# Attention block with a mixture of experts: blanks in 19 pieces with result rows of their own, scatters without pauses, the last group's chain dealt anew, joins in 5 parts, mixed order

## The reference

```
h = layernorm(x) * (1 + ca) + sa
q, k, v = split(h @ W_attn + b_attn)                      # 16 heads of 8 channels
att = softmax(q k^T / sqrt(8) + slope_head * (s - t), s <= t only)
x = x + ga * ((att v) @ W_proj + b_proj)
h = layernorm(x) * (1 + cb) + sb
probs = softmax(h @ router_w^T)                           # 8 experts
w, e = top 2 of probs;  w = softmax(w)
y_e = expert_scale[e] * (silu(h @ w1[e]^T) @ w2[e]^T)     # 512 hidden values
x = x + gb * (w_0 y_e0 + w_1 y_e1)
```

## Time and profile before

| | us |
|---|---|
| median of 3 runs | 574.66 (572.46 to 578.66) |
| profiled execution, its own time | 576.61 |
| its span, first to last instruction | 574.8 |
| mean granted clock of PE | 0.919 |
| busy PE, DVE, ACT, POOL | 477.8, 442.8, 384.1, 181.6 |

### The profile page before, as it was taken

The page is one execution under the profiler, slowest core; times in us unless marked ns, Lnnn a source line. Parts: engine busy times, 40 slices in busy tenths (PEclk is TensorE's granted clock), DMA queues, the critical chain, the costliest instruction groups (busy, mean ns, idle before and its releaser), DMA issues.

```text
span 574.8 us, 15827 instructions
## 1 busy us (share of the span) xinstructions
PE 477.8 (83%) x6215; PEld 261.2 (45%) x6215; DVE 442.8 (77%) x760; ACT 384.1 (67%) x747; POOL 181.6 (32%) x336
## 2 busy tenths in 40 slices
PE   3756888889999999999999999998996597799900
PEld 2422333344353454344354344345333587799800
DVE  3689899989999998999998999973877368343303
ACT  3932266668989889889898889886875363355400
POOL 3410000010113111410034101093088857666660
PEclk9965599999999999999999999999879599799965
DMA  5592112000012555242400000100221311122106
GB/s 158 180 325 66 30 34 52 1 3 4 7 35 42 144 234 226 82 157 53 80 10 3 4 2 7 30 7 22 92 71 39 80 53 43 52 66 59 43 22 219
DMA packets 31658, 40.78 MB, mean 71 GB/s; under 512 B 6348, under 2 KB 26768, under 8 KB 30313
## 3 DMA queue, kind: packets, MB, share of 16 engines
q1 hardware_dynamic: 28976, 35.12, 20.8%
q0 software_dynamic: 2272, 4.24, 2.1%
q10 hardware_dynamic: 336, 0.42, 0.2%
HBM read 19.17 MB, written 20.84 MB: 70 GB/s over the span
## 4 chain that ended last, share of the span: by engine, by line
PE 32%; POOL 17%; DVE 12%; issue 7%; ACT 5%; DMA 3%; SPq 1%; POOLq 0%; ACTq 0%; DVEq 0%
PE pv L772 14%; PE b L806 8%; DVE part L1045 8%; POOL y_scratch L1565 6%; PE b L735 5%; POOL slot_scratch L1558 4%; POOL pause L1537 4%; ACT probs L1382 3%; PE b L708 2%; DMA raw<-y_scratch 1%; ACT raw L1349 1%; PE b L884 1%; DMA inverse<-inverse_scratch 1%; POOL raw L1516 1%; POOL yn L1518 1%
## 5 line engine op out<-in xcount | busy, mean ns | idle before, releaser
L1382 ACT ACTIVATE probs<-b 128x512 f32<-128x512 f32 (+1 forms) x576 | 296.1, 571 | 71.3 <-PE b L806 33.8
L1045 DVE TENSOR_REDUCE part<-b 128x2 f32<-128x1024 f32 (+2 forms) x320 | 322.5, 1060 | 21.4 <-PE b L735 9.5
L772 PE MATMUL pv<-probs,v_cur 128*32 128x256 f32 (+1 forms) x2432 | 178.3, 376 | 0.0
L806 PE MATMUL b<-aug 55*128 55x256 bf16 (+1 forms) x1216 | 127.9, 268 | 12.2 <-ACT probs L1382 11.6
L735 PE MATMUL b<-aug 52*128 52x512 bf16 (+3 forms) x640 | 118.1, 367 | 18.6 <-DVE part L1045 16.5
L806 PEld LDWEIGHTS b<-aug 55*128 55x128 bf16 x1216 | 44.5, 95 | 123.9 <-ACT probs L1382 111.0
L772 PEld LDWEIGHTS pv<-probs,v_cur 128*32 128x32 f32 x2432 | 50.4, 109 | 58.5 <-ACT probs L1382 31.3
L735 PEld LDWEIGHTS b<-aug 52*128 52x128 bf16 x640 | 34.6, 95 | 37.4 <-DVE part L1045 27.4
L1565 POOL DMA_INDIRECT y_scratch<-aug,xt x39 | 39.1, 1002 | 30.3 <-POOL pause L1537 30.3
L901 PE MATMUL b<-w2T_sb,hst 128*128 x312 | 43.4, 285 | 3.5 <-DVE aug L1222 2.7
L884 PE MATMUL b<-hTt,aug 128*128 128x128 f32 x312 | 45.0, 291 | 0.0
(11 more groups left out here) (185 smaller groups left out, 375.9 us busy)
## 6 DMA issues: line engine op xcount, KB each, us to landing
slot_scratch<-blank SPq DMA_DIRECT2D x8, 1040.0 KB, 6.7
xt<-slot_scratch SPq DMA_DIRECT2D x39, 65.0 KB, 1.9
aug<-q_scratch SPq DMA_DIRECT2D x6, 384.0 KB
aug<-k_scratch SPq DMA_DIRECT2D x6, 384.0 KB
w2T_sb<-in_w2T SPq DMA_DIRECT2D x1, 2048.0 KB, 10.3
aug<-in_w1T SPq DMA_DIRECT2D x8, 256.0 KB, 2.7
raw<-y_scratch SPq DMA_DIRECT2D x4, 512.0 KB, 5.5
q_scratch<-pieces SPq DMA_DIRECT2D x4, 384.0 KB, 2.6
```

The source lines that it names most:

```text
L772: return mm(pv[32 * hh:32 * hh + 32, c0:c1], v_cur[:, kb, hh, :], probs[:, step_ % 2, hh, at_:at_ + c1 - c0], start=(kb == 0 and c0 == 0), ...
L806: ins = mm(bank[:, at_:at_ + w], k_aug[g % 2][n, pair, kb * P:kb * P + P], q_aug[g % 2][n, pair, j * CW + c0:j * CW + c1], start=True, sto ...
L1045: ins = nc.vector.tensor_reduce(dst, b1[:, slot:slot + 2, at_:at_ + w], AX.X, ALU.max)
L1382: nc.scalar.activation(out, b2[:, (n2 - 1) % RING2, 0:PAIRS * w].rearrange("p (b t) -> p b t", b=PAIRS), ACT.Exp).then_inc(exp_done, 1)
```

## The change

- `blank` is used as two halves. POOL gives every blank row a number of its own, TOPK * T and up, for one of 19 pieces at a time (`number_blanks`), after the transfer of the piece two before has landed; SP sends a piece at each of 19 steps of group 1. `y_scratch` grows from 4,096 to 23,296 rows, `slot_scratch` from 16,512 to 19,200, and the scatter has no bounds check.
- No pause stands ahead of sends and scatters.
- In the last group projections, deviations, routing and counts stand at other steps, and DVE's order is written anew; the send of chunk 0 stands ahead of the deviation of chunk 2. List 1 is made within the tile loop. The late parts of chunk 3 stand one tile earlier.
- The inverse of the sums is taken two steps earlier in each group.
- The end has five parts, of 4, 4, 4, 2 and 2 blocks of 128 tokens.
- In groups 1 to 3, in the steps that hold no diagonal block (24 of 36), one maxima task is interleaved with the scores on PE.

```diff
-SUMS_OUT, SUMS_IN, INVERT, INVERSE_OUT, INVERSE_IN = 3, 4, 8, 9, 10
+SUMS_OUT, SUMS_IN, INVERT, INVERSE_OUT, INVERSE_IN = 3, 4, 6, 7, 8
...
-TABLES_AT, EMPTY_AT, BLANK_AT = 5, [6, 7], [11, 12, 13, 15, 18, 22, 24, 29, 31]
+TABLES_AT, EMPTY_AT = 5, 6
+BLANK_AT = [7, 8, 9, 10, 11, 12, 13, 14, 15, 16, 18, 19, 21, 22, 23, 24, 25, 26, 28]
...
-DEVIATION_AT = {19: 0, 20: 1}
-PROJECT = {16: 0, 18: 1, 23: 2}
+DEVIATION_AT = {17: 0, 20: 1}
+PROJECT = {16: 0, 19: 1, 24: 2}
...
-COUNT = {24: 0, 27: 1, 31: 2}
+COUNT = {21: 0, 26: 1, 33: 2}
...
-SLOT_ROWS = SPARE + P
+SLOT_ROWS = SPARE + MOST * P
...
-PAUSE, GATHER_PAUSE = 512, 224
...
-LATE_PROJECT, LATE_RESIDUAL, LATE_TOKENS, LATE_TURN, LATE_LOGITS, LATE_KEEP = 2, 2, 3, 5, 5, 5
-LATE_EXP, LATE_ROUTE, LATE_COUNT = 6, 6, 8
+LATE_PROJECT, LATE_RESIDUAL, LATE_TOKENS, LATE_TURN, LATE_LOGITS, LATE_KEEP = 1, 1, 2, 4, 4, 4
+LATE_EXP, LATE_ROUTE, LATE_COUNT = 5, 5, 7
+MORE_LIST = {0: (0, 1), 1: (2, 3)}
...
-SENDS_AFTER = 6
+SENDS_AFTER = 5
+LAST_JOINS = [(0, TPC), (TPC, 2 * TPC), (2 * TPC, 3 * TPC), (3 * TPC, NT - 2), (NT - 2, NT)]
...
-        y_dram = nc.dram_tensor("y_scratch", (TOPK * T, C), fp32, kind="Internal").ap()
+        y_dram = nc.dram_tensor("y_scratch", (TOPK * T + SLOT_ROWS, C), fp32, kind="Internal").ap()
...
+                        q = BLANK_AT.index(p)
+                        q0, q1 = HELD * q, min(HELD * (q + 1), EACH)
+                        sp.wait_ge(empty_s, q + 1)
+                        sp.dma_start(slot_dram.rearrange("(p q) c -> p (q c)", p=P)[:, q0 * ROW:q1 * ROW], blank[:, CHUNK * (q % 2):CHUNK * (q % 2) + (q1 - q0) * ROW]).then_inc(blank_out[q % 2], 16)
...
-                def scores_then_maxima(p, b, upto):
-                    alternate(scores(p, b, 0), scores(p, b, 1))
+                def scores_and_maxima(p, b, upto):
+
+                    k, (j, kbs) = at[0], STEPS[p]
+                    if k < upto and not first and kbs[0] < TPC * j:
+                        alternate(chain(scores(p, b, 0), maxima(k, 0, False, True)), chain(maxima(k, 1, True, False), scores(p, b, 1)))
+                        at[0] += 1
+                    else:
+                        alternate(scores(p, b, 0), scores(p, b, 1))
                     pass1(upto)
...
-            list_all(1)
             for j in range(DEEP - 1):
                 stage(j)
...
+                for piece in MORE_LIST.get(j, ()):
+                    list_tiles(1, piece)
...
-            def space_out(columns):
-
-                own.inc(nc.gpsimd.memset(pause[:, 0:columns], 0.0))
-                own.wait()
+            def number_blanks(q):
+
+                if q >= 2:
+                    pool.wait_ge(blank_out[q % 2], 16 * (q // 2))
+                numbers = blank[:, CHUNK * (q % 2):CHUNK * (q % 2 + 1)].rearrange("p (n c) -> p n c", c=ROW)[:, :, 1:2].bitcast(mybir.dt.uint32)
+                nc.gpsimd.iota(numbers, [[1, HELD], [0, 1]], base=TOPK * T + HELD * q, channel_multiplier=EACH).then_inc(empty_s, 1)
...
                 pool.wait_ge(yt_s, j + 1)
-                space_out(GATHER_PAUSE)
                 to = xt[:, j % ROWS_DEEP, 1:2].bitcast(mybir.dt.uint32)
-                nc.gpsimd.indirect_dma_start(y_dram, bass.IndirectOffsetOnAxis(ap=to, axis=0), yt[:, j % OUT_DEEP, :], None, bounds_check=TOPK * T - 1, oob_is_err=False).then_inc(tile_out(j)[0], 16)
+                nc.gpsimd.indirect_dma_start(y_dram, bass.IndirectOffsetOnAxis(ap=to, axis=0), yt[:, j % OUT_DEEP, :], None).then_inc(tile_out(j)[0], 16)
...
+            send_chunk(0)
             deviation(2)
-            for c in range(3):
-                send_chunk(c, PAUSE)
+            send_chunk(1)
+            send_chunk(2)
```

More of the change, by code:

```diff
@@ L13 @@
 from contextlib import ExitStack
-from itertools import zip_longest
+from itertools import chain, zip_longest
 import numpy as np
@@ L397, in build @@
         y_out = [sem(f"y_out{k}") for k in range(OUT_DEEP)]
-        y_in = [sem(f"y_in{c}") for c in range(NC_)]
+        y_in = [sem(f"y_in{m}") for m in range(len(LAST_JOINS))]
         joined = sem("joined")
@@ L831, in step @@
                                 take(pe, rows_in[j % 2], HG * 16)
-                            scores_then_maxima(p, b, min(PLAN[first][p][b], NTASK) if last else PLAN[first][p][b])
+                            scores_and_maxima(p, b, min(PLAN[first][p][b], NTASK) if last else PLAN[first][p][b])
                             if p not in START:
@@ L1222, in keep, with join @@
                 V.scalar_tensor_tensor(yt[:, j % OUT_DEEP, :], b1[:, 2 + j % 2, 0:C], xt[:, j % ROWS_DEEP, 0:1], gate[:, 1, :], ALU.mult, ALU.mult).then_inc(yt_s, 1)
[L1224 to L1229 removed]
+            def join(m):
+                n0, n1 = LAST_JOINS[m]
+                xc = x_sb[:, n0:n1, :]
+                dve.wait_ge(y_in[m], 16)
+                step(V.tensor_tensor(xc, xc, yfin[:, n0:n1, 0, :], ALU.add))
+                V.tensor_tensor(xc, xc, yfin[:, n0:n1, 1, :], ALU.add).then_inc(joined, 1)
             residual(0)
@@ L1233, in _ @@
             residual(1)
-            scale_tokens(1)
             keep_logits(0)
             route(0, 0)
+            scale_tokens(1)
+            for k in range(1, 5):
+                route(0, k)
+            keep_logits(1)
+            route(1, 0)
+            place(0)
+            scale_of(0)
+            weights(0)
             scale_sums(2)
             add_sums(2)
-            keep_logits(1)
-            route(1, 0)
-            for k in range(1, 5):
-                route(0, k)
-            residual(2)
-            place(0)
-            scale_tokens(2)
-            scale_of(0)
-            weights(0)
             for k in range(1, 5):
                 route(1, k)
-            keep_logits(2)
-            route(2, 0)
+            residual(2)
             place(1)
@@ L1286, in _ @@
             keep(TILES - 1)
-            for c in range(NC_):
-                join(c)
+            for m in range(len(LAST_JOINS)):
+                join(m)
         @block.scalar
@@ L1576, in group @@
                             tables()
-                        if p in EMPTY_AT:
-                            q = CHUNK * EMPTY_AT.index(p)
-                            own.inc(nc.gpsimd.memset(blank[:, q:q + CHUNK], 0.0))
+                        if p == EMPTY_AT:
+                            own.inc(nc.gpsimd.memset(blank[:, :], 0.0))
                             own.wait()
-                            numbers = blank[:, q:q + CHUNK].rearrange("p (n c) -> p n c", c=ROW)[:, :, 1:2].bitcast(mybir.dt.uint32)
-                            own.inc(nc.gpsimd.iota(numbers, [[0, TOPK * TPC], [0, 1]], base=TOPK * T, channel_multiplier=0))
-                        if p == EMPTY_AT[-1]:
-                            own.wait()
-                            nc.gpsimd.memset(tick[:, 7:8], 0.0).then_inc(empty_s, 1)
+                        if p in BLANK_AT:
+                            number_blanks(BLANK_AT.index(p))
                         if p == BIAS_AT[0] - 1:
```

74 lines of the change are left out of this document (33 added, 41 removed).

## The result

The median fell from 574.51 to 555.98 us (551.65 to 558.35 over 4 runs); the ratio to the kernel before is 0.966, its 95% interval 0.958 to 0.974. That is a gain of 18.5 us where 27.2 were forecast. The profiled execution has a span of 553.9 us, 6.3 above the forecast sum of 547.6; the median lies 8.5 above the forecast 547.5.

What follows compares the result with a forecast made beforehand. No one engine was taken to bind the whole: PE in middle groups, sends before the experts, POOL's scatters at the end. Last scatter 533.5 plus 14.1 gave 547.6, 27.2 below 574.8; median 574.66 - 27.2 = 547.5 us, range 535 to 560.

Steps and rivals of the forecast that it cites:

- (a): Mixed order of scores and maxima on PE in three groups: gain of 0.5 us per group, -1.5 in all.
- (b): Last group's chain dealt anew: -1 us of a possible 7.3, as moved steps are late as often as early.
- (c): Start of the tile loop: tile 0 starts as attention ends, tile 6 at 462.7 instead of 468.23, gain 5.5 us.
- (d): Tiles 6 to 10, chunk 3's routing: unchanged at 12.5 us, so tile 10 starts at 475.2.
- (e): Tiles 10 to 38: 54.1 us at about PE's own pace instead of 62.8; last up-projection at 529.3.
- (f): Scatters and sends on POOL: 1.1 us each instead of 2.06 between scatters; last scatter at 533.5, not 559.96.
- (g): Blanks numbered in 19 pieces in group 1, and the sums' inverse taken two steps earlier: no cost, 0 us.
- (h): End, from the last scatter's start: 14.1 us instead of 14.84, as the last join handles two token blocks.
- POOL did not keep its wait: First rival, scatters on POOL: the 0.77 us wait belongs to the scatter, not the pause; +5.8, 553 us; chance 0.10.
- scatters did not go by landing: Rival on POOL's queue: each transfer must land before the next, 2.4 us each, 584 us; chance 0.06.
- the numbering did not hold up the maxima: Rival in group 1: waiting for blank pieces to land delays the maxima, +9 us, 556.5 us; chance 0.08.
- the deal cleared nothing: Rival in the last group: the new deal clears all of the 7.3 us instead of 1, 541 us; chance 0.10.

Runs made afterwards that it cites:

- Scaling first: The changed kernel with POOL's second scaling of the last values moved ahead of the first deviation, one step earlier: 551.2 us.
- the projection at step 18: The changed kernel with POOL's second scaling ahead of the first deviation, plus chunk 1's projection one step earlier, at step 18 as before: 547.93 us.
- the plain order: The changed kernel with scores and maxima on PE in the order of before, not interleaved: 555.91 us against 555.98.
- the best version: The changed kernel with POOL's second scaling ahead of the deviation, chunk 1's projection at step 18 and late parts one tile later, routing in one piece: 544.23 us.
- the routing in halves: The best version with chunk 3's routing in two pieces, parts 1 to 3 behind one tile and the rest behind the next: 544.32 us.

## Why the prediction was right, and where not

The time lay in the range and the sign was right, and most of the mechanism: the experts begin when attention ends, POOL no longer lags at the end, and PE sets the pace from tile 10 on. Two of the tests that were to show it wrong came out against it: attention ended later than 440, tile 10 started later than 480. Two of its signs failed by less: scatters stood 1.26 apart where POOL was behind, not 1.0 to 1.2, and the group with the blanks was 0.9 longer than the next.

- (a) and (b) put the last value product at 437.9; it ended at 442.07, 4.2 late. The miss is larger: group 1 began at 165.78 instead of 168.40, 2.6 earlier by chance, since no edit touches what is ahead of it. (a) was small, 0.3 to 0.4 in group 2. The step that failed is (b): "the moved steps are late by a step or two as often as early", so -1. The last group became 4.0 longer. Scaling first took 4.4 of its 99.3 away, the projection at step 18 another 2.7: both shown by a run, with the clock behind each wait in the figure. The order of the change showed POOL's two scalings behind the first deviation, where DVE's tokens start, and I did not ask what shares their time. "What is behind it isn't delayed" was nearly right: the eight sends took 10.6 us, and PE waited 0.91 for the turn of chunk 2.
- (c) was right as a sum: tokens 17.2 us behind the last product (17.7 forecast), tile 6 25.3 (24.8). One reading in it was wrong: of the 8.9 us of waits, 1.05 end at 467.23, behind the stretch from 446.43 to 465.59, so 7.9 were to be taken off. And the 5 us standstill in it was taken as the price of uncovered DVE work. It was the price of one table: with the late parts one tile later, tile 10 comes 6.4 us sooner while the tokens stay where they are.
- (d) was taken as unchanged, 12.5 us; it took 482.13 - 467.36 = 14.8. Behind the same 2.7 us wait PE ran at 0.50 for 5.5 us, which it had not done before, where the same product took 1.15 us instead of 2.07:

```profile
479.41 1.15 PE L901 MATMUL b<-w2T_sb,hst 128*128 x8 [2.72 <-DVE aug L1222]
```

With the scaling and the projection moved, the same loop kept its clock behind this wait (1.00 from 466.6 to 472.1) and took 36.0 - 23.5 = 12.5.
- (e) 53.2 against 54.1, and the last scatter 3.9 us behind the last up-projection against 4.2: right.
- (f) 1.26 us per scatter where 1.1 was taken; 1.26 is the middle value that I had worked out from the sends and passed over. The sends of chunk 3 began at 476.75, not near 471.5, a value for which the prediction gives no working. POOL caught up not at once but at 507.76, which cost nothing.
- (g) the blanks cost nothing, shown above within a microsecond; the earlier inverse was not run by itself. (h) 14.7 against 14.1.

The terms' errors, 4.2 + 0.5 + 2.3 - 0.9 - 0.3 + 0.6 = 6.4, make up the span's 6.3; without the 2.6 of luck ahead of group 1 they are 8.9, near the 8.5 by which the median is off. The rivals: POOL did not keep its wait, scatters did not go by landing, and the numbering did not hold up the maxima; the deal cleared nothing, as it stood. As for scatters beside a copy of weights, which the first rival names: the 13 from 509.65 to 532.40 each have a copy of 0.43 us on DVE within their issue and take 0.96, not 1.19.

What no step asked is which part carries the gain. The pauses alone gave 27.0; that this is almost the 27.2 forecast for the whole is chance. The rest took 7.8 back, through the late parts one tile early (6.4), the scaling behind the deviation (4.8) and the projection one step late (3.3). These three add up to more than the 11.8 that undoing them together gave, and with them undone the remaining parts are worth some 4.0.

## What to carry to other kernels

When a wait is to be removed, remove it by itself first and read the trace before anything else is moved: here the old tables, untouched, fitted the kernel without pauses better than the new ones. An instruction that is moved ahead of its input can become one that its engine stands still for, as PE did here for 5.43 us ahead of the turn of chunk 3. Look for work on POOL and DVE that becomes simultaneous when one of the two is moved (here four token instructions took 3.35 us beside POOL's scaling and 1.4 without it), and price the wait on the engine behind both (PE, 2.17 us).

## What the runs showed of the hardware

- A DVE tensor_scalar of 128 x 256 float32 that started 0.06 us behind a POOL tensor_tensor of 128 x 512 (1.27 us) took 1.36 us; with none beside them four took 0.41 each.
- Indirect transfers of 128 rows started 1.26 us apart on POOL where it was behind, scatters with a bounds check 1.29, though each landed a median of 2.3 to 2.4 us after its issue: they overlapped. Behind a memset of 224 columns and a wait for it scatters started 1.54 apart, with a bounds check 2.06.
- A copy of 0.43 us on DVE that began within the issue of a scatter left it at 0.96 us (13 times in the change, 509.65 to 532.40). Where one of 0.41 to 0.43 began 0.04 to 0.16 ahead of an indirect transfer, that took 1.10 to 1.21 (459.46, 479.41, 494.77), and 1.19 in the kernel before (copy at 503.51, scatter at 503.60).
- The same wait did not always go with a low clock. PE's granted clock was 0.50 behind waits of 5.43 us (460 to 468) and 2.72 (476.5 to 482) in the change, and 1.00 behind the wait of 2.72 in the kernel before (479.4 to 493), which had 0.50 behind waits of 0.95 (421 to 425) and 2.91 (496 to 501.5). The wait of 2.17 in the last group was followed by 0.62 in the change and by 1.00 with the plain order. Behind the wait of 2.66 the next up-projection took 1.68 us in the best version, and 1.12 with the routing in halves. What decides it no run here shows.
